# Half-width gates over six slots, a projection over two, bulk transfers on a second queue, and experts from slot 1

## The reference

```python
x  = x + attn0(xn, ...) + (silu(xn @ wg.T) * (xn @ wu.T)) @ wd.T      # 384 hidden
xn = layernorm(x)
probs = softmax(xn @ gate_w.T);  top_p, top_i = top_k(probs, 2)
rank  = cumsum(one_hot(top_i)) - 1;  keep = rank_of_token < capacity
out   = sum_e comb[:, e] * ((silu(xn @ gp[e].T) * (xn @ up[e].T)) @ down[e].T)
x  = x + masked_attn(xn, ...) + out
```

## Time and profile before

| | |
|---|---|
| median of 3 runs | 544.76 us (542.74 to 545.1) |
| profiled execution | 544.03 us, span 542.0 us |
| TensorE, VectorE, ScalarE, GpSimd busy | 84%, 74%, 61%, 48% |
| mean granted TensorE clock | 0.950 |
| moved by DMA | 48.27 MB, mean 89 GB/s |

### The profile page before, as it was taken

The page is one execution under the profiler, slowest core; times in us unless marked ns, Lnnn a source line. Parts: engine busy times, 40 slices in busy tenths (PEclk is TensorE's granted clock), DMA queues, the critical chain, the costliest instruction groups (busy, mean ns, idle before and its releaser), DMA issues.

```text
span 542.0 us, 9302 instructions
## 1 busy us (share of the span) xinstructions
PE 454.8 (84%) x3394; PEld 169.4 (31%) x3394; DVE 400.5 (74%) x538; ACT 328.8 (61%) x422; POOL 262.5 (48%) x499
## 2 busy tenths in 40 slices
PE   3456979889988999899989898987899999999952
PEld 1101213224322433242312431221245453455511
DVE  5699778886998699869887798789876777623204
ACT  2102666776677667656676577777766567667560
POOL 6861263724425562886378657884201233163240
PEclk9755889999999999999999999999999999999995
DMA  3896596244511360626252645174731111010018
GB/s 82 238 230 89 89 343 106 93 163 146 90 43 61 118 62 4 66 72 127 25 52 39 157 43 56 41 160 68 109 52 32 45 50 50 4 44 25 21 47 219
DMA packets 143742, 48.27 MB, mean 89 GB/s; under 512 B 109890, under 2 KB 139090, under 8 KB 142866
## 3 DMA queue, kind: packets, MB, share of 16 engines
q1 hardware_dynamic: 141394, 42.93, 38.1%
q0 software_dynamic: 2304, 4.76, 2.6%
HBM read 22.81 MB, written 23.14 MB: 85 GB/s over the span
## 4 chain that ended last, share of the span: by engine, by line
PE 53%; DVE 18%; issue 10%; ACT 10%; DMA 4%; SPq 4%; POOL 1%; POOLq 0%; ACTq 0%; DVEq 0%
PE ps L763 14%; DVE mx L1114 11%; PE ps L747 9%; PE ps L732 7%; ACT PT L962 6%; PE ps L802 3%; PE ps L810 3%; PE ps L785 2%; PE ps L803 2%; SPq L433 2%; PE ps L693 2%; PE ps L825 2%; PE ps L822 2%; PE ps L786 1%; DVE th L1135 1%
## 5 line engine op out<-in xcount | busy, mean ns | idle before, releaser
L1114 DVE TENSOR_REDUCE mx<-ps 128x2 f32<-128x1024 f32 x256 | 309.4, 1223 | 73.1 <-PE ps L732 65.1
L962 ACT ACTIVATE PT<-ps 128x1024 f32<-128x1024 f32 x256 | 258.6, 1026 | 125.9 <-PE ps L747 116.5
L763 PE MATMUL ps<-PT,Vp 128*32 128x512 f32 x1024 | 138.1, 611 | 5.4 <-ACT PT L962 4.4
L732 PE MATMUL ps<-KO,QO 48*128 48x512 bf16 (+1 forms) x512 | 104.5, 406 | 39.7 <-ACT PT L962 22.6
L747 PE MATMUL ps<-QO,KO 59*128 59x512 bf16 x512 | 100.2, 390 | 3.8 <-DMA QO<-mT 2.5
L520 POOL DMA_INDIRECT y_tokens<-expert_io,meta x40 | 38.6, 964 | 71.5 <-ACT expert_io L994 48.5
L747 PEld LDWEIGHTS ps<-QO,KO 59*128 59x128 bf16 x512 | 24.6, 93 | 142.8 <-issue 87.9
L1135 DVE SCALAR_TENSOR_TENSOR th<-th,ps 128x320 f32<-128x320 f32 (+1 forms) x44 | 23.8, 541 | 35.2 <-ACT th L978 29.4
L732 PEld LDWEIGHTS ps<-KO,QO 48*128 48x128 bf16 (+1 forms) x512 | 25.6, 96 | 70.9 <-ACT PT L962 38.6
L545 POOL CAST mp<-mx 128x32 bf16<-128x32 f32 x16 | 3.4, 214 | 82.9 <-DVE mx L1114 78.7
L509 POOL DMA_INDIRECT x_places<-xe,place_i x32 | 31.9, 995 | 22.3 <-ACT PT L962 15.2
(11 more groups left out here) (166 smaller groups left out, 475.1 us busy)
## 6 DMA issues: line engine op xcount, KB each, us to landing
z<-part SPq DMA_DIRECT2D x16, 384.0 KB
z<-part SPq DMA_DIRECT2D x16, 256.0 KB
QO<-z SPq DMA_DIRECT2D x64, 48.0 KB
KO<-z SPq DMA_DIRECT2D x64, 48.0 KB
x_places<-expert_io SPq DMA_DIRECT2D x2, 1300.0 KB, 7.4
expert_io<-x_places SPq DMA_DIRECT2D x8, 320.0 KB, 3.5
QO<-z SPq DMA_DIRECT2D x6, 384.0 KB
KO<-z SPq DMA_DIRECT2D x6, 384.0 KB
```

What stands on the lines that cost most here:

```text
L732: mm = pe.matmul(ps[:, 2 * pair + half, :], rows_of(QO[u % 3], half, 2 * s + jj, rows, (qt, qt + 1)), rows_of(KO[u % 3], half, 2 * s + jj, ...
L763: last = pe.matmul(ps[32 * g:32 * g + 32, PV_BANK, :], Vp[u % 2][:, k, head(s, g), :], PT[:, (2 * t + g % 2) % 4, g // 2, :], start=(s % 2 ...
L962: act.activation(PT[:, e % 4], ps[:, 2 * pair:2 * pair + 2, :], ACT.Exp).then_inc(exp_done, 1)
L1114: dve.tensor_reduce(mx[:, a, qt, col:col + 5:4], ps[:, 2 * pair:2 * pair + 2, :], AX_X, ALU.max, negate=True).then_inc(max_read, 1)
```

## The change

The gates of layer 0 are computed for 256 tokens at a time, in six slots, 10 to 15, in place of three. For units that follow a layer 0 unit, the projection's four tiles come two in slot 6 and two in slot 7, with the residual in slot 8 and the statistics behind its second maximum. The rank products go to slot 5 beside the transposes of the maxima, into the other half of `SIDE`, with their copy in slot 6. The loads and `empty_places` are issued by ScalarE. The last unit's places and scatters come earlier on GpSimd, the experts start in slot 1 of unit 6, the results are sent earlier, and the first results are added ahead of the last normalization.

```diff
-        EXPERTS_FROM = 4
+        EXPERTS_FROM = 1
+        G0, N_TOK0, GATE_SLOT = 2 * HB, S // 2, SLOTS_U - 2 * HB
+        def spread(u):
+            return u >= 1 and layer(u - 1) == 0
-            return HB * u + slot - 9 if u < B and 9 <= slot < 9 + HB else None
+            return G0 * u + slot - GATE_SLOT if u < B and slot >= GATE_SLOT else None
...
-            if u < 2:
-                empty_places(sp, u)
...
-        def scatter(pool, p, tiles, u, slot):
+        def scatter(pool, p, tiles, u, slot, each=2):
-                pool.wait_ge(exp_done, 2 * (SLOTS_U * u + slot + i) + 1)
+                pool.wait_ge(exp_done, 2 * (SLOTS_U * u + slot) + each * i + 1)
...
             if u == U - 1:
-                send_results(pool, 2)
+                send_results(pool, 3)
+                send_results(pool, 4)
...
                 parts(pool, p, 1)
-                if spread:
+                if p == U - 1:
+                    places_of(pool, p, route)
+                    scatter(pool, n, (3,), u, 8, each=1)
+                    scatter(pool, p, (0, 1), u, 9, each=1)
+                elif spread:
                     scatter(pool, n, (3,), u, 7)
...
-            if p < U and layer(p) == 1:
+            if p < U - 1 and layer(p) == 1:
                 places_of(pool, p, route)
...
                 send_results(pool, 0)
-            if p == U - 1:
-                scatter(pool, p, (0,), u, 10)
+                send_results(pool, 1)
             if n < U:
                 split_max(pool, n, 0)
             if u == U - 2:
-                send_results(pool, 1)
+                send_results(pool, 2)
...
-                scatter(pool, p, (1, 2, 3), u, 12)
+                scatter(pool, p, (2, 3), u, 12, each=1)
...
-            u, i = g // HB, g % HB
+            u, i, c = g // G0, g % G0 // 2, g % 2
...
-            cols = slice(i * P, (i + 1) * P)
-            pe.matmul(ps[:, 2 * pair, :], wg[:, cols], xnT[u % 4][:], start=True, stop=True).then_inc(gate_ps[0], 1)
+            cols, x_T = slice(i * P, (i + 1) * P), xnT[u % 4][:, c * N_TOK0:(c + 1) * N_TOK0]
+            pe.matmul(ps[:, 2 * pair, 0:N_TOK0], wg[:, cols], x_T, start=True, stop=True).then_inc(gate_ps[0], 1)
...
                 max_transposes(pe, u, 1)
+                if p < U and layer(p) == 1:
+                    rank_mms(pe, p)
             if slot == 6 and u >= 1:
-                out_mms(pe, w, (2, 3))
-            if slot == 7 and p < U and layer(p) == 1:
-                pe.wait_ge(unit_done, u)
-                rank_mms(pe, p)
+                out_mms(pe, w, (1,) if spread(u) else (2, 3))
+            if slot == 7 and spread(u):
+                out_mms(pe, w, (3,))
...
-                    out_mms(pe, u - 1, (0, 1))
+                    if u + 2 < U and layer(u + 2) == 1:
+                        pe.wait_ge(rank_read, seq(u + 2) + 1)
+                    out_mms(pe, u - 1, (0,) if spread(u) else (0, 1))
+                if slot == 7 and spread(u):
+                    out_mms(pe, u - 1, (2,))
...
                     maxima_copy(act, u, 1)
+                    if p < U and layer(p) == 1:
+                        ranks_copy(act, p)
...
                 exponential(act, 2 * t + 1)
+                if slot == 9 and u < 2:
+                    empty_places(act, u)
...
-                if slot == 7 and u >= 1:
+                if slot == (8 if spread(u) else 7) and u >= 1:
                     residual(dve, w)
...
         def last_vector(dve):
+            add_results(dve, 0)
             normalize_out(dve, U - 1, 1)
-            for b in range(B):
+            for b in range(1, B):
                 add_results(dve, b)
...
-            for dst, src in loads:
-                sp.dma_start(dst, src).then_inc(loaded, 16)
...
-            for e in range(3, E):
+            for e in range(5, E):
                 send_results(pool, e)
...
             qk_copy(act, 1, 1, SIDE)
+            for dst, src in loads:
+                act.dma_start(dst, src).then_inc(loaded, 16)
```

More of the change, by code:

```diff
@@ L336, in across @@
             return ps[:, 2 * pair:2 * pair + 2, :].rearrange("p k n -> p (k n)")[:, a:z]
-        def empty_places(sp, part):
-            sp.wait_ge(empty_ready, part + 1)
-            if part == 0:
-                for k in range(2):
-                    sp.dma_start(y_tokens[k * T:(k + 1) * T].rearrange("(p m n) d -> p m (n d)", p=P, n=8),
-                                 fill_zero.unsqueeze(1).to_broadcast([P, T // P // 8, 8 * D])).then_inc(emptied, 16)
-            first = part * (E // 2) * PLACES
-            sp.dma_start(x_places[first:first + E // 2 * PLACES].rearrange("(e p j) d -> p e (j d)", p=P, j=JE),
-                         fill.rearrange("p (e n) -> p e n", e=E // 2)).then_inc(emptied, 16)
         N_EMPTIED = 16 * 4
@@ L780, in gate_up_0 @@
         def gate_up_0(pe, g):
-            u, i = g // HB, g % HB
+            u, i, c = g // G0, g % G0 // 2, g % 2
             pe.wait_ge(ready, 1)
             pair = take_pair(pe, "gate0", g)
-            cols = slice(i * P, (i + 1) * P)
-            pe.matmul(ps[:, 2 * pair, :], wg[:, cols], xnT[u % 4][:], start=True, stop=True).then_inc(gate_ps[0], 1)
-            pe.matmul(ps[:, 2 * pair + 1, :], wu[:, cols], xnT[u % 4][:], start=True, stop=True).then_inc(up_ps[0], 1)
+            cols, x_T = slice(i * P, (i + 1) * P), xnT[u % 4][:, c * N_TOK0:(c + 1) * N_TOK0]
+            pe.matmul(ps[:, 2 * pair, 0:N_TOK0], wg[:, cols], x_T, start=True, stop=True).then_inc(gate_ps[0], 1)
+            pe.matmul(ps[:, 2 * pair + 1, 0:N_TOK0], wu[:, cols], x_T, start=True, stop=True).then_inc(up_ps[0], 1)
         def places_mms(pe, e):
@@ L818, in out_mms @@
                 if L == 0:
-                    pe.wait_ge(h_ready[0], HB * (u + 1))
+                    pe.wait_ge(h_ready[0], G0 * (u + 1))
             for t in tiles:
@@ L839, in rank_mms @@
             n_oh = NT * 2 * E
-            pe.matmul(ps[:, SIDE, 0:n_oh], tri[:], oh2, start=True, stop=True)
-            pe.matmul(ps[:, SIDE, n_oh:2 * n_oh], ones_bf[:], oh2, start=True, stop=True).then_inc(rank_ps, 1)
+            pe.matmul(ps[:, SIDE, S // 2:S // 2 + n_oh], tri[:], oh2, start=True, stop=True)
+            pe.matmul(ps[:, SIDE, S // 2 + n_oh:S // 2 + 2 * n_oh], ones_bf[:], oh2, start=True, stop=True).then_inc(
+                rank_ps, 1)
         def side_mms(pe, u, slot):
@@ L876, in side_mms @@
                 pe.wait_ge(unit_done, u)
-                if p < U and layer(p) == 1:
-                    pe.wait_ge(rank_read, seq(p) + 1)
                 v_mms(pe, n, SIDE)
@@ L970, in half_tanh @@
         def half_tanh(act, L, g):
-            n = S if L == 0 else HALF
+            n = N_TOK0 if L == 0 else HALF
             act.wait_ge(gate_ps[L], g + 1)
@@ L1016, in ranks_copy, with empty_places @@
                 act.wait_ge(place_ready, seq(u))
-            act.copy(ranks[:].rearrange("p i t k -> p (i t k)"), ps[:, SIDE, 0:4 * NT * E]).then_inc(rank_read, 1)
+            act.copy(ranks[:].rearrange("p i t k -> p (i t k)"), ps[:, SIDE, S // 2:S // 2 + 4 * NT * E]).then_inc(rank_read, 1)
+        def empty_places(act, part):
+            act.wait_ge(empty_ready, part + 1)
+            if part == 0:
+                for k in range(2):
+                    act.dma_start(y_tokens[k * T:(k + 1) * T].rearrange("(p m n) d -> p m (n d)", p=P, n=8),
+                                 fill_zero.unsqueeze(1).to_broadcast([P, T // P // 8, 8 * D])).then_inc(emptied, 16)
+            first = part * (E // 2) * PLACES
+            act.dma_start(x_places[first:first + E // 2 * PLACES].rearrange("(e p j) d -> p e (j d)", p=P, j=JE),
+                         fill.rearrange("p (e n) -> p e n", e=E // 2)).then_inc(emptied, 16)
         def scalar_unit(act, u):
@@ L1037, in scalar_unit @@
                     maxima_copy(act, n, 0)
-                if slot == 8 and p < U and layer(p) == 1:
-                    ranks_copy(act, p)
                 exponential(act, 2 * t + 1)
+                if slot == 9 and u < 2:
+                    empty_places(act, u)
                 if slot == 0 and u >= 1:
@@ L1131, in gated @@
         def gated(dve, L, g):
-            n, bank = S if L == 0 else HALF, 2 * pair_of(f"gate{L}", g)
+            n, bank = N_TOK0 if L == 0 else HALF, 2 * pair_of(f"gate{L}", g)
             t = th[:, g % 2, 0:n]
@@ L1139, in gated @@
             if L == 0:
-                if g % HB == 0 and g > 0:
-                    dve.wait_ge(y_ps, g // HB)
-                dst = h0_T[:, g % HB, :]
+                if g % G0 == 0 and g > 0:
+                    dve.wait_ge(y_ps, g // G0)
+                dst = h0_T[:, g % G0 // 2, g % 2 * N_TOK0:(g % 2 + 1) * N_TOK0]
             else:
@@ L1191, in vector_unit @@
                     normalize_out(dve, w, 1)
-                if slot == 7 and u >= 1:
+                if slot == (8 if spread(u) else 7) and u >= 1:
                     residual(dve, w)
-                if slot == 8 and f < U:
```

(3 more changed lines are left out.)

2 lines of the change are left out of this document (1 added, 1 removed).

## The result

| | before | after |
|---|---|---|
| median (4 runs each, same chip) | 544.36 us (542.74 to 545.1) | 559.65 us (559.56 to 559.9) |
| profiled execution, span | 544.03, 542.0 us | 559.58, 557.6 us |

The ratio is 1.0292, 95% interval 1.0271 to 1.0312: 15.3 us slower. The forecast was 549.1 with a range to 556.0; the direction was right, the size missed the range.

What follows compares the result with a forecast made beforehand. TensorE (84%) and VectorE (74%) were taken as nearly full together in gated slots, neither alone setting the time. Terms 1.4 + 1.5 - 1.2 - 0.6 - 0.6 + 9.8 - 6.0 = +4.3 gave median 549.1 us, range 541 to 556.

Steps and rivals of the forecast that it cites:

- bulk transfers: Start: loads on a second queue delay the first score product 4.6 and operands 0.5, give back 3.7; +1.4 us.
- emptying on ScalarE: Unit 0, after slot 9's second exponential: three issues hold ScalarE 2.3 us, 0.8 of it idle; +1.5 us (0 to 4.1).
- half gates: Slots 10 to 15 of layer 0 units: PSUM pair held half as long; 0.3 us per unit, four units, -1.2.
- projection and ranks: Projection over slots 6 and 7, ranks in slot 5: -0.15 us per unit each, four units, -0.6 each.
- experts from slot 1 and tail: Unit 6 slot 1: TensorE waits 8.5 us for block 0, loop end +9.8; last residual directly follows projection, -6.0.
- earlier scatters: GpSimd, unit 5: the last unit's places and scatters end in slot 14; only helps if something waited; no term.
- worst case of 8.1: Start: if moved transfers hold everything behind them, unit 1's writes and reads end 8.1 us later, at 54.6.
- The part given back, 3.7: Slot 8 of unit 0: 2.55 us wait for maxima rows gone, plus 1.2 for the half clock behind it.
- The rival that fills the idle time: Layer 0 units: finer pieces fill TensorE's gaps to the cap, 7.8 us less than forecast, 541.3; chance 0.20.
- its list: Chances: forecast 0.45, TensorE gaps filled 0.20, SP queue not delayed 0.18, longer SP and ScalarE holds 0.12, no net effect 0.05.

Runs made afterwards that it cites:

- d1: The kernel before with only the seventeen loads issued by ScalarE behind its copies for unit 1; 544.8 us, ratio 1.0101 to before.
- f1: The kernel before with only the emptying issued by ScalarE in slot 9 of units 0 and 1; 539.48 us, ratio 1.001 to before.
- y1: The kernel before with only the half gates in slots 10 to 15; 536.4 us, ratio 0.9931 to before.
- c5: The kernel before with half gates, projection over slots 6 and 7, ranks in slot 5 and emptying on ScalarE; 537.68 us, ratio 0.9974 to before.
- s2: The kernel after with loads on SP, experts from slot 4, and six early scatters split into four and two; 538.69 us, ratio 0.9984 to before.
- e1: The kernel after with only its row of six scatters split into four and two; 553.7 us, ratio 1.0251 to before.
- d4: The kernel before with half gates and the three large expert weight loads issued by SP in unit 1; 533.91 us, ratio 0.9895 to before.
- y3: The kernel before with only the rank products beside the transposes of the maxima; 539.92 us, ratio 1.0011 to before.
- d3: The kernel before with experts from slot 1, results sent earlier and first results added ahead of the last normalization; 544.64 us, ratio 1.0097 to before.
- x3: The kernel after with the last unit's places and scatters ordered on GpSimd as in the kernel before; 557.82 us, ratio 1.0253 to before.
- x4: The kernel after with experts from slot 4, results and additions as before, scatters still early; 553.99 us, ratio 1.0193 to before.
- c1_three: The kernel after with loads back on SP, first places ahead of unit 7's second row reads, and last unit's scatters in old slots; 550.59 us, ratio 1.0122.
- x1: The kernel after with the seventeen loads back on the SP queue, emptying still on ScalarE; 555.52 us, ratio 1.0204 to before.
- x2: The kernel after with the first two expert blocks' place loads ahead of unit 7's second row reads on SP; 553.78 us, ratio 1.018 to before.

## Why the prediction was wrong

By its own steps, with the single-part run that measured each:

| step | forecast | measured |
|---|---|---|
| bulk transfers | +1.4 | +5.2 (d1), 6.0 in its trace |
| emptying on ScalarE | +1.5 | 0 to +1 (f1) |
| half gates | -1.2 | -2.8 by the medians, -3.7 by the ratio (y1) |
| projection and ranks | -1.2 | about +1.8 (lags of c5, s2, e1 against y1, d4); ranks alone 0 (y3) |
| experts from slot 1 and tail | +9.8 - 6.0 | +5.0 (d3): 10.8 and -6.5 |
| earlier scatters | 0 ("only helps") | 5.4 in the trace of after; without them x3 is 4.8 ahead at (7,12), 1.8 in the medians |

- **Wrong: bulk transfers.** The step took one queue of bytes, 9.5 us of transfers against 1.4 of free room, and moved only unit 1's transfers and the maxima rows by it. It left out layer 0's feed-forward weights (`ffn_loads`), which the SP queue asks for at 27.79 to 29.49, behind the moved loads in time, and it left out that GpSimd converts them before it splits the first maxima. So 6.6 and 4.1 us follow one another, where I counted 4.6 and took a worst case of 8.1. The part given back, 3.7, was right: slots 7 and 8 gave 3.4.
- **Wrong: "that only helps if something waited for them".** The earlier scatters were costed at nothing. In after they went with the stand in unit 5, and with pairs in their place (x3) it was gone. It could not be read from a row of the profile shown, but the same effect was there in small, 0.3 to 0.8 us in the slots with scatters.
- **Right: experts from slot 1.** The place (SP's sixteen row reads) was right, and the wait (8.5 forecast, 7.07 and a clock at 0.50 for 10 us), the end of the loop and the tail (both by d3) came within 1.5 us of the forecast. Block 0 came later than the 392.4 that I gave, since all ahead of it was later.
- **Undersized: half gates.** The 0.3 us a unit came in slots 9 to 15 of units 1 and 2, not of 3 and 4. That it comes from a shorter hold of PSUM was argued and not tested. The 0.37 us in slot 0 of each next unit were not in the sum, and why they come was not traced. The rival that fills the idle time was half right here, though not enough to outweigh the rest.
- **Not borne out: projection and ranks**, -0.6 each: they cost about 1.8 us, in slots 5 to 8. TensorE's idle time that they were to fill was not gained; what makes these slots longer was not traced. The emptying's +1.5 was 0 to 1 alone (f1), and more in x4, where the DMA engines were 0.77 to 1.04 busy.

Loads, emptying, half gates, spread with ranks, and experts sum to 5.2 + 0.5 - 2.8 + 1.8 + 5.0 = 9.7 us (0.5 taken for the emptying), and with unit 5's 5.4 to 15.1 of the 15.3. That close a sum is largely luck. With the half gates by their ratio it is 14.2; or, with the stand at what x3 kept in its median, 1.8, it is 11.5. And e1_after_four_two has no stand in unit 5 and is still 14.1 us slower than the kernel before beside it. There the parts cost 4 us more together than one by one, 2.0 in unit 0 (lag at (1,0) 8.0 against 6.0 in d1) and 1.5 in the first expert slots (18.6 against 17.1 in d3). What is shown is which parts lose and where; how the 15.3 us divide among them is known to a few microseconds only.

The prediction's chances by outcome (slower 0.49, same 0.27, faster 0.24) do not follow from its list, which gives 0.46, 0.31 and 0.23 with each rival at its own number; nothing else hangs on them.

## What to carry to other kernels

When a bulk transfer is moved earlier, list every transfer that is asked for after it until it has landed, and follow each to its first reader: the one that hurts need not be on the queue that was in view. When work that waits for data is moved earlier, move the transfer's place in its queue first, and check what that place itself waits for (c1_three). And test a change of several parts by single parts: here one part of five made a faster kernel, and with the large weights loaded a unit later it gave 5.7 us.

## What was not expected of the hardware

- While GpSimd issues indirect DMAs one after the other, the other engines can start late on work whose inputs are done: by 0.70 us at a row of five in before, and by 2.10 us at the end of a row of six in x4_experts4 (373.68 to 375.78), with the clock at 0.65 and then 0.50 in the next two windows of 2 us. In other groups of runs a row of five cost 0.03 us there and a row of six nothing. It goes with the 4 us between the groups for the unchanged kernel. The Trainium skill (SBUF — State Buffer, the passage on the "DVE blocks DMA" trap) describes another case, GpSimd kept from writing its descriptors while VectorE runs certain operations; no run here shows that.
- The last slots, with neither maxima nor experts, can fall to the lower clock: slots 12 to 14 of unit 7 lost 3.2 to 3.3 us in the traces of x1, x2 and x3 and 0.8 in after. In x2 and x3 the fall came behind an exponential that ScalarE began only after 1.7 us of idle time, beside a row of result scatters; in e1_after_four_two it idled 0.57 there. The runs of x1 spread from 553.82 to 559.03, those of after, with as many such slots, from 559.56 to 559.9: such slots alone do not make a kernel unsteady.
